# Moving VectorE's row maximum and second-norm rows inside the steps of an attention round

## What is computed

```
def layernorm(x): return (x - mean(x)) / sqrt(var(x) + 1e-5)

q      = einsum(layernorm(x) @ Wq.T, w_kc_q)         # 16 heads
scores = einsum(q @ W_qr, rope(ctx) @ W_kr)          # b, 16 heads, 128, 128
attn   = softmax(scores)
out    = einsum(attn @ rope(ctx), w_kc_kv) @ Wo.T
x1     = x + tanh(g_xattn) * out
h      = layernorm(x1)                               # the second norm
y      = moe_top2_of_8(h) + shared_mlp(h)
result = x1 + tanh(g_ffn) * y
```

## Time and profile before

| | us |
|---|---|
| median of 3 runs | 2029.69 |
| lowest and highest of them | 2027.64, 2030.72 |
| the profiled execution | 2027.22 |
| its span, first to last instruction | 2025.4 |
| PE busy | 1915.3 (95%) |
| DVE busy | 871.0 (43%) |
| POOL busy | 715.9 (35%) |
| ACT busy | 666.0 (33%) |
| mean granted clock of TensorE | 0.984 |

### The profile page before, as it was taken

How to read it: one execution, slowest core, us unless ns; L and a number is a source line. 1 busy time by engine, 2 the same in 40 slices (tenths; PEclk the granted TensorE clock), 3 DMA queues, 4 the chain that set the end, 5 groups by cost and what they waited for, 6 DMA issues and landing times.

```text
span 2025.4 us, 32045 instructions
## 1 busy us (share of the span) xinstructions
PE 1915.3 (95%) x11801; PEld 1070.0 (53%) x11972; DVE 871.0 (43%) x1674; ACT 666.0 (33%) x1905; POOL 715.9 (35%) x779
## 2 busy tenths in 40 slices
PE   7799999999999988899999999999999999999999
PEld 7455555555555555444445555555554444444444
DVE  5655555555555555446642222222223433233243
ACT  5655555555555555522012222222210000000000
POOL 5655555555555565610023333343302110110101
PEclk9899999999999999999999999999999999999999
DMA  9445544444444555451329999999943522221202
GB/s 297 115 102 102 102 102 99 105 102 102 102 102 102 110 123 117 102 137 46 106 65 203 235 248 222 213 219 218 207 101 125 114 73 49 77 83 27 78 19 86
DMA packets 427300, 250.01 MB, mean 123 GB/s; under 512 B 360369, under 2 KB 366257, under 8 KB 427185
## 3 DMA queue, kind: packets, MB, share of 16 engines
q1 hardware_dynamic: 415664, 210.61, 44.5%
q0 software_dynamic: 11520, 37.76, 6.7%
HBM read 113.02 MB, written 48.23 MB: 80 GB/s over the span
## 4 chain that ended last, share of the span: by engine, by line
PE 56%; DVE 14%; issue 11%; ACT 9%; POOL 6%; DMA 2%; SPq 1%; DVEq 0%; POOLq 0%; ACTq 0%
PE score L725 11%; PE o L815 8%; PE score L804 7%; PE p_bank L725 5%; PE m_bank L725 5%; PE o L737 5%; ACT arena L892 5%; DVE arena L1015 4%; PE p_bank L804 4%; PE m_bank L804 4%; PE c_bank L737 3%; PE t_bank L737 3%; DVE arena L1090 3%; POOL arena L1384 2%; DVE arena L1141 1%
## 5 line engine op out<-in xcount | busy, mean ns | idle before, releaser
L583 PE MATMUL o<-arena 128*128 128x512 bf16 x1473 | 338.9, 379 | 4.7 <-DVE arena L1015 1.0
L892 ACT ACTIVATE arena<-score,arena 128x128 f32<-128x128 f32 x512 | 181.5, 367 | 268.7 <-DVE arena L1090 268.7
L725 PE MATMUL score<-arena 128*128 128x512 bf16 x1037 | 235.9, 381 | 2.6 <-DMA arena<-xn_d 1.3
L583 PEld LDWEIGHTS o<-arena 128*128 128x128 bf16 x1536 | 150.3, 99 | 155.0 <-DVE arena L1015 1.7
L1379 POOL TENSOR_TENSOR arena<-arena 128x512 bf16<-128x512 f32 x128 | 150.2, 1174 | 208.7 <-ACT arena L845 206.0
L632 PE MATMUL p_bank<-arena 128*128 128x256 bf16 x1536 | 195.4, 288 | 0.9 <-DVE arena L1015 0.9
L725 PEld LDWEIGHTS score<-arena 128*128 128x128 bf16 x1056 | 103.7, 98 | 128.1 <-issue 3.1
L632 PEld LDWEIGHTS p_bank<-arena 128*128 128x128 bf16 x1536 | 153.7, 103 | 32.9 <-DVE arena L1015 1.6
L1470 POOL TENSOR_TENSOR arena<-arena 128x1088 bf16<-128x1088 f32 x32 | 71.9, 2248 | 274.9 <-ACT arena L922 274.9
L815 PE MATMUL o<-arena 128*128 128x512 bf16 (+1 forms) x681 | 160.0, 379 | 2.0
L1015 DVE TENSOR_TENSOR arena<-arena 128x512 bf16<-128x512 f32 (+2 forms) x219 | 152.4, 705 | 17.1 <-ACT arena L932 5.0
(11 more groups left out here) (161 smaller groups left out, 2739.8 us busy)
## 6 DMA issues: line engine op xcount, KB each, us to landing
xrow_d<-arena SPq DMA_DIRECT2D x80, 256.0 KB, 3.7
arena<-w_expert SPq DMA_DIRECT2D x32, 544.0 KB, 5.3
arena<-w_shared SPq DMA_DIRECT2D x22, 384.0 KB, 3.5
arena<-x SPq DMA_DIRECT2D x16, 512.0 KB, 4.1
arena<-x SPq DMA_DIRECT2D x32, 256.0 KB, 4.2
x_d<-arena SPq DMA_DIRECT2D x32, 256.0 KB, 2.4
xn_d<-arena SPq DMA_DIRECT2D x32, 256.0 KB, 2.2
arena<-x_d SPq DMA_DIRECT2D x8, 1024.0 KB, 6.5
```

Of the source, the lines that this page charges most:

```text
L583: mm = pe.matmul(o_bank[b % 2][:, :], lhsT=cT[u % 2][:, a, h, :], rhs=M_w[:, w, head_of(hg, h), :], start=(hg == 0 and n == 0), stop=(hg = ...
L725: mm = pe.matmul(dst[:, :], lhsT=wsh[m][:, a, col:col + P], rhs=xs[g % 2][:, w, t, :], start=(n == 0), stop=(n == 3 * KT - 1))
L892: mm = act.activation(prob[:, u % 4, h, :], score_bank[u % 2][:, h * S:(h + 1) * S], ACT.Exp, bias=neg_max[:, u % 4, h:h + 1], accum_out=d ...
```

## The change

Two things are moved on VectorE; no instruction is added or left out, and the other engines' programs are the same.

- In odd steps the row maximum stands ahead of the residual x1. That alters something in steps 3 and 7 of a round only, since the other odd steps have no x1.
- The second norm's rows, both batches at the end of step 2 before, are now made one batch a step: that of the first batch in step 2 and that of the second in step 3, both behind the low part of the context (and, in step 2, the row maximum) and ahead of the low part of the piece.

```
                 links(*((1,) if m == 0 else ()))
+                if k % 2 == 1:
+                    row_max(k + 6, it)
                 if k % 4 == 3 and within(k // 4, NB):
...
                     dve.scalar_tensor_tensor(out=x1[b % 4], in0=o_bank[b % 2][:, :], scalar=tanh_sb[:, 0:1],
                                              in1=x1[b % 4], op0=ALU.mult, op1=ALU.add).then_inc(x1_done, 1)
-                if k % 2 == 1:
-                    row_max(k + 6, it)
                 u = k + 2
...
                 if k % 2 == 0:
                     row_max(k + 6, it)
+                if m in (2, 3):
+                    norm_2(m - 2, g2, g1, it)
                 q = k + 12
...
                 if m == 1:
                     norm_1(g1, it)
-                if m == 2:
-                    norm_2(g2, g1, it)
...
-            def norm_2(g2, g1, it):
+            def norm_2(s, g2, g1, it):
                 if within(g2, NG):
+                    b = 2 * g2 + s
                     wait(dve, rsqrt_step, RSQRT_OPS * (g1 + 1), 2 * RSQRT_OPS, it)
-                    for s in range(2):
-                        b = 2 * g2 + s
-                        wait(dve, xn2_lo, b - 1, 4, it)
-                        wait(dve, l2_mm, b - 1, 4, it)
-                        dve.tensor_scalar(xn2[:, s, :], x1[b % 4], mean_var[:, s, 0:1], rstd[:, s:s + 1],
-                                          ALU.subtract, ALU.mult).then_inc(xn2_ready, 1)
+                    wait(dve, xn2_lo, b - 1, 4, it)
+                    wait(dve, l2_mm, b - 1, 4, it)
+                    dve.tensor_scalar(xn2[:, s, :], x1[b % 4], mean_var[:, s, 0:1], rstd[:, s:s + 1],
+                                      ALU.subtract, ALU.mult).then_inc(xn2_ready, 1)
```

## The result

| | before | changed |
|---|---|---|
| median, us | 2028.93 (4 runs) | 1972.59 (4 runs) |
| lowest and highest, us | 2027.64, 2030.72 | 1972.50, 1974.21 |
| profiled execution, us | 2027.22 | 1972.50 |
| its span, us | 2025.4 | 1970.7 |
| mean granted clock | 0.984 | 0.994 |

The ratio is 0.9724, with a 95% interval of 0.9707 to 0.9740. The gain is 56 us; 47 were forecast, and the time lies 3.4 us under the lower end of the range.

What follows compares the result with a forecast made beforehand. TensorE, busy 95% of the span, was taken as the bound, stalled by VectorE's chain. From 2027.2 us profiled, 28.7 of waits and 18.3 of clock left 1980.2; with 2.5 for the median, 1983 us, range 1976 to 2003.

Steps and rivals of the forecast that it cites:

- The bottleneck and the chain: Each round TensorE's step 4 scores wait, mostly 3.64 us, on VectorE; work ahead of step 3's row maximum is paid in full.
- the regular rounds: Rounds 1 to 11, each standing still 3.63 or 3.64 us at the scores: 1.9 us saved per round, 20.9 us in all.
- the 2.41 us: How much earlier step 3's row maximum comes: 1.77 us from moving both norm rows, 0.64 from moving the residual.
- The disputed cost: Second norm row in step 3, ahead of the piece's low part, on TensorE's path: taken as 0.5 us.
- The rival with that name: GpSimd goes first at step 3's second norm row, which then costs 1.4 us every round: 1992 to 2011 us, chance 0.08.
- Rounds 12 to 14: Late rounds' waits at the scores: 2.85 us saved in each of 12 and 13, 1.5 us in round 14.
- The clock: TensorE's clock falls after the scores' wait in most rounds; with shorter waits no round falls, saving 18.3 us.
- The rival with the clock still falling: TensorE's clock still falls behind the scores' wait in many or all rounds: 1988 to 2001 us, chance 0.15.
- the sentence on step 7: Step 7's row maximum comes 0.64 us earlier, but TensorE does not wait in that step: nothing gained.

Runs made afterwards that it cites:

- e3: The kernel before with only the norm rows moved, the row maximum of odd steps left where it was: 1994.2 us, ratio 0.9837.
- e4: The kernel before with only the row maximum put ahead of the residual in step 3: 2013.0 us, ratio 0.9924.
- e8: The changed kernel with the second batch's norm row put back at the end of step 2: 1990.1 us, ratio 0.9804.
- e5: The changed kernel with the second norm row moved behind the low part of the piece in step 3: 1969.6 us, ratio 0.9715.
- e2: The kernel before with only the row maximum put ahead of the residual in step 7: 2029.3 us, ratio 0.9999.
- e1: The changed kernel with the residual put back ahead of the row maximum in step 7: 1978.1 us, ratio 0.9757.

## Why the prediction was right, and where it was wrong

*The bottleneck and the chain* were read rightly. The wait at the scores fell from 3.64 to 1.68 us in the regular rounds (forecast: to about 1.7), and e3 and e4 gave the waits that their parts of the 2.41 us call for: 3.64 - 0.64 = 3.0 (2.98 measured) and 3.64 - 1.23 = 2.4 (2.34).

*The disputed cost,* the second norm row in front of the piece, came at 0.54 us where 0.5 was taken, by the order that had been worked out. e8 and e5 show what would have been had GpSimd been first: 1.38 and 1.28. The rival with that name had the right mechanism and price, and did not occur.

*Rounds 12 to 14* were undersized. The row took at most 0.64 us in rounds 12 and 13 and 0.80 in round 14, where I took 0.95 and 1.4. The waits fell by 3.34, 3.23 and 2.17 us where 2.85, 2.85 and 1.5 were forecast: 1.5 us more in all. The regular rounds gave 0.06 us each more than the 1.9 forecast, 0.7 us in all. Together with the regular rounds, 52.7 - 22.4 = 30.3 us of waiting at the scores went in rounds 1 to 14, and 28.1 were forecast.

*The clock* kept to its higher level behind the wait of every round, as forecast: 18.3 us. The rival with the clock still falling was given 0.15. It did not occur, but the margin was small and part of this is luck: the forecast leaned on a round that kept the clock after 2.66 us and one that kept it after 1.88, and in other kernels a wait of 2.66 us (e2, round 14, granted clock 0.80 in the 8 us window) and one of 1.88 (e3, round 0, 0.79) lost it. The changed kernel waits 1.7 to 1.8 us.

*The step that failed* is the sentence on step 7, "TensorE does not wait in it: nothing". It put the term at nothing because it looked for a wait in step 7 alone. The row maximum of step 7 comes 0.64 us earlier, and with it the work of ScalarE and GpSimd behind it; in step 0 GpSimd's series then leaves VectorE's small operation free, the row maximum of step 0 comes 0.4 us earlier, and the chain from there ends at the piece of step 3, where TensorE waited for VectorE. That wait stood in the earlier trace rows, where its bracket shows 0.30 us, and was left out of the sum. e1 measures the term: 6.1 us. With it the rounds add up: 30.3 + 18.3 + 6.1 = 54.7 us, against 54.35 measured.

*The whole miss.* Of the 10.4 us between 1983 and 1972.6, 6.1 are the swap in step 7, 2.2 the waits at the scores that were undersized, and 2.4 the step from the profiled run to the median, below; together these are 0.3 us more than the miss, and what offsets them is not shown.

*The range.* Its lower end, 1976, was the forecast's own with a few us off. It took in every way in which the gain could be smaller and none in which it could be greater. The 2.5 us between the profiled run and the median of before were carried over too, and the changed kernel has a difference of only 0.1 us. In the gain by medians, 56.3 us, 1.6 us come from that.

## What to carry to other kernels

In a hand-ordered pipeline, what stands on an engine ahead of the instruction that another engine's long step waits for is paid in full; what stands between the request and its answer is free. Look for such a place in every step, and follow a saved half microsecond through the following steps until a wait of the bound engine or a gap absorbs it; that this step's own wait is zero says nothing. Follow the other engines too: here VectorE's lead was absorbed by a gap, and the gain came back because GpSimd was earlier as well. Where a wait of TensorE is followed by slow matmuls, price the wait with them, and do not judge a change of a few tenths of a us by the total while they are there.

## What the runs showed of the hardware

The table shows how often the granted clock fell at a wait of a given length. The wait comes once a round, between stretches in which TensorE is busy all but throughout. The rounds are 1 to 11 except where noted, in one trace of each kernel:

| wait, us | kernel | rounds with a fall |
|---|---|---|
| 1.2 | e5 | 0 |
| 1.7 | changed, e1 (rounds 1 to 12) | 0 of 12 each |
| 1.88 | before, e2, e3, round 0 of each | 1 of 3 (e3) |
| 2.34 | e3, rounds 1 to 13 | 1 of 13 |
| 2.5 | e8 | 2 |
| 2.66 | before, e2, round 14 of each | 1 of 2 (e2) |
| 2.98 | e4 | 5 |
| 3.64 | before | 9 |
| 3.64 | e2 | 9 |

I had expected a wait either to cost the clock or not; in these traces it is a chance that rises with the length, from none at 1.7 us to nine in eleven at 3.6. The counts are rough, since runs of one kernel differ (e3, above), and a wait of 1.88 us was once enough. Nor is 1.7 us shown to be safe: one run of e1 took 1985 us at a mean clock of 0.992, where the traced one took 1977 at 0.995. A fall cost between 1.3 and 2.5 us. So e4, which took 0.66 us off a wait of 3.64, won 15.6 us, of which 9.9 are the waits at the scores (55.9 to 46.0) and the rest the clock.

Two VectorE operations from SBUF to SBUF took longer beside GpSimd, and ended only when the GpSimd instruction that had started before them was over, whatever their own size: 1.38 us (e8) and 1.28 us (e5) instead of 0.54 for 128x512 elements, and 0.65 instead of 0.17 for 128x4 (e1 and the changed kernel in step 0). They ended 0.29, 0.27 and 0.02 us behind the GpSimd instruction. The Trainium skill's page "SBUF — State Buffer", in the section on the two separate sides, has this as an exclusive lock on a shared pair of ports, held for the whole instruction. The rows agree that the second one waits, but it ends sooner behind the first than its own full time alone. What I had not expected is that the smallest operations are hit the hardest for their size, and that 0.1 us in the order of arrival moves 0.4 us of a round.
